# Q projection: weights by a cast on ScalarE from plain f32 loads instead of casting DMAs

## The reference

```python
x = x + attn(layernorm(x), Wq, Wk, Wv, Wo)      # 8192 tokens, H = 4096
x = x + ffn(layernorm(x), int4 gate, up, down)  # inner size 11008

# inside attn; 32 query heads, 8 key/value heads, head size 128
q = hidden_states @ Wq                          # [8192, 4096] @ [4096, 4096]
q = q * cos + rotate_half(q) * sin              # rotary embedding
# k, v alike; window of 512 past tokens; softmax; probs @ v; @ Wo
```

## Time and profile before

| what | us |
|---|---|
| median of the two runs shown | 10358.07 |
| the two runs | 10188.14 and 10528.0 |
| the profiled execution, its device time | 10198.96 |
| the profiled execution, span of its slowest core (core 2) | 10197.4 |
| spans of all cores in it | 10127.5 to 10197.4 |
| Q projection, first to last matmul start on core 2 | 3741.8 to 4577.9 |

### The profile page before, as it was taken

One profiled execution on the slowest core, in us unless ns is written; L12 is line 12 of the kernel. 1 busy time (PEld: TensorE's weight loads), 2 busy tenths in 40 slices (PEclk: granted clock), 3 DMA queues, 4 the chain that ended last, 5 costly groups with the idle time before them and its releaser, 6 DMA issues.

```text
span 10197.4 us, 80736 instructions; the slowest of 8 cores (10127.5 to 10197.4 us)
## 1 busy us (share of the span) xinstructions
PE 5936.4 (58%) x29632; PEld 2963.5 (29%) x29632; DVE 2148.5 (21%) x6972; ACT 2092.0 (21%) x4186; POOL 267.1 (3%) x316
## 2 busy tenths in 40 slices
PE   0000000332244566666657757999978879999886
PEld 0000000222222242221126633444433334444333
DVE  4555555444412112221100021000000000000000
ACT  3444444666603000004430031000000000000000
POOL 0000000000000001110000000000000000000000
PEclk9999999555566787776668868999989989999998
DMA  9999999999843334330024415777744467777333
GB/s 292 325 324 325 324 323 287 271 273 262 250 62 79 37 42 40 39 37 0 0 33 75 78 35 116 145 152 149 151 129 141 132 133 152 150 152 148 139 135 119
DMA packets 2257604, 1544.43 MB, mean 151 GB/s; under 512 B 1632064, under 2 KB 2095936, under 8 KB 2200640
## 3 DMA queue, kind: packets, MB, share of 16 engines
q1 hardware_dynamic: 1911968, 1134.47, 44.3%
q0 software_dynamic: 308096, 134.24, 9.9%
q10 hardware_dynamic: 37152, 270.55, 6.7%
HBM read 983.41 MB, written 295.70 MB: 125 GB/s over the span
## 4 chain that ended last, share of the span: by engine, by line
PE 50%; DMA 30%; DVE 7%; ACT 6%; issue 4%; SPq 2%; POOL 1%; ACTq 0%; DVEq 0%; POOLq 0%
PE pd L1074 12%; DMA scr_g<-wb_g 11%; PE pgg L1001 10%; PE puu L1009 10%; DMA qsl_d<-qd_in 7%; PE pq L679 5%; PE po L855 5%; DVE wb_g L247 3%; ACT wb_d L385 3%; DMA wq_sl<-wq_t 2%; DMA wgu_sl<-scr_u 2%; DMA x1t_sl<-scr_x1t 2%; PE pvv L569 2%; DMA wo_sl<-wo_t 2%; ACT probs L777 2%
## 5 line engine op out<-in xcount | busy, mean ns | idle before, releaser
L324 PE MATMUL ptd<-ident,wb_d 128*128 128x128 bf16 x2752 | 302.6, 308 | 2452.5 <-ACT wb_d L385 2452.5
L1074 PE MATMUL pd<-hT,wd_sl 128*128 128x512 bf16 x5504 | 1209.8, 383 | 258.6 <-DVE out_st L1090 238.2
L1001 PE MATMUL pgg<-x2nT,wgu_sl 128*128 128x512 bf16 x5504 | 1223.7, 381 | 108.5 <-DMA wgu_sl<-scr_u 99.0
L1009 PE MATMUL puu<-x2nT,wgu_sl 128*128 128x512 bf16 x5504 | 1216.0, 379 | 0.0
L324 PEld LDWEIGHTS ptd<-ident,wb_d 128*128 128x128 bf16 x2752 | 283.8, 145 | 2471.0 <-issue 2471.0
L276 ACT ACTIVATE wb_u<-qsl_u,nzs_u,s_u 128x128 bf16<-128x128 int32 x1892 | 737.0, 479 | 918.1 <-DMA qsl_u<-qu_in 918.1
L247 DVE TENSOR_SCALAR wb_g<-qsl_g,s_g,nzs_g 128x128 bf16<-128x128 int32 x2752 | 713.2, 344 | 732.5 <-DMA scr_g<-wb_g 730.2
L1074 PEld LDWEIGHTS pd<-hT,wd_sl 128*128 128x128 bf16 x5504 | 542.9, 99 | 925.5 <-issue 289.4
L1001 PEld LDWEIGHTS pgg<-x2nT,wgu_sl 128*128 128x128 bf16 x5504 | 536.4, 98 | 775.8 <-issue 146.3
L1009 PEld LDWEIGHTS puu<-x2nT,wgu_sl 128*128 128x128 bf16 x5504 | 538.6, 98 | 649.3
L679 PE MATMUL pq<-x1nT_o,wq_sl 128*128 128x512 bf16 x2048 | 522.0, 423 | 325.1 <-DMA wq_sl<-wq_t 325.1
(11 more groups left out here) (96 smaller groups left out, 3048.4 us busy)
## 6 DMA issues: line engine op xcount, KB each, us to landing
qsl_g<-qg_in SPq DMA_DIRECT2D x86, 2048.0 KB, 37.4
qsl_u<-qu_in SPq DMA_DIRECT2D x86, 2048.0 KB, 44.3
qsl_d<-qd_in SPq DMA_DIRECT2D x86, 2048.0 KB, 16.7
wd_sl<-scr_d SPq DMA_DIRECT2D x80, 2048.0 KB, 8.7
scr_u<-wb_u ACTq DMA_DIRECT2D x86, 1024.0 KB, 18.3
scr_g<-wb_g ACTq DMA_DIRECT2D x86, 1024.0 KB, 27.5
scr_d<-sst ACTq DMA_DIRECT2D x86, 1024.0 KB, 11.4
wq_sl<-wq_t POOLq DMA_DIRECT2D x128, 256.0 KB, 5.7
```

Source lines behind the costliest of these rows:

```text
L324: last = tensor.transpose(ptd[it % 2][:, hs * 128:(hs + 1) * 128], wb_d[it % 2][:, hs * 128:(hs + 1) * 128], ident[:])
L1001: last = tensor.matmul(pgg[it % 2][:], wgu_sl[2 * (it % 2)][:, ht * 128:(ht + 1) * 128], x2nT[:, ht * TOK + tc * 512:ht * TOK + (tc + 1) * ...
L1009: last = tensor.matmul(puu[it % 2][:], wgu_sl[2 * (it % 2) + 1][:, ht * 128:(ht + 1) * 128], x2nT[:, ht * TOK + tc * 512:ht * TOK + (tc + ...
L1074: last = tensor.matmul(pd[:, oi * 512:(oi + 1) * 512], wd_sl[(og * NGRP + grp) % 2][:, gi * 1024 + oi * 128: gi * 1024 + (oi + 1) * 128], ...
```

## The change

The host lays Wq out as [32 heads, 4 quarters, 128 partitions, 1024], so that what one partition needs of a quarter is one run of 4 KB. The loads move from GpSimd's queue to SyncE's and stay f32: each quarter is loaded in two halves of [128, 512] f32 (256 KB) into one of two staging tiles `wqf0` and `wqf1`. ScalarE copies each half into `wq_sl` and casts it to bf16 on the way. A load into a staging tile waits until the copy that read it two units earlier is done (`aQC`). The first copy of a head waits until both halves of the head before are done (`pQ`). TensorE waits for all eight copies of its head. GpSimd does nothing in this stage. The matmuls and the rotary embedding stay as they are.

```diff
-    wq_t = dram_in("wq_t", [NH, H, 128], F32)
+    wq_t = dram_in("wq_t", [NH, 4, 128, 1024], F32)
@@
     wq_sl = [P.sb(f"wq_sl{i}", [128, 8 * 128], BF16, OFF_G + i * 2 * KB) for i in range(4)]
+    wqf = [P.sb(f"wqf{i}", [128, 512], F32, OFF_G + 12 * KB + i * 2 * KB) for i in range(2)]
...
-    def p4_gp(gpsimd):
-        P.wge(gpsimd, "pVb", 32)
-        q = 0
-        for qt in range(NH):
-            for quarter in range(4):
-                if q >= 4:
-                    P.wge(gpsimd, "pQ", 2 * ((q - 4) // 4) + 2)
-                P.inc(gpsimd.dma_start(
-                    wq_sl[q % 4].ap().rearrange("p (t q) -> p t q", q=128),
-                    wq_t[qt].rearrange("(a t p) q -> a p t q", a=4, p=128)[quarter]),
-                    "lq%d" % (q % 4), 16)
-                q += 1
+
+    def p4_sync(sync):
+        P.wge(sync, "pVb", 32)
+        for u in range(8 * NH):
+            qt, a, hf = u // 8, (u % 8) // 2, u % 2
+            if u >= 2:
+                P.wge(sync, "aQC", u - 1)
+            P.inc(sync.dma_start(
+                wqf[u % 2][:],
+                wq_t[qt, a, :, hf * 512:(hf + 1) * 512]), "lqf%d" % (u % 2), 16)
+
+    def p4_sca(scalar):
+        P.wge(scalar, "pVb", 32)
+        for u in range(8 * NH):
+            qt, a, hf = u // 8, (u % 8) // 2, u % 2
+            P.wge(scalar, "lqf%d" % (u % 2), (u // 2 + 1) * 16)
+            if u % 8 == 0 and qt >= 1:
+                P.wge(scalar, "pQ", 2 * qt)
+            P.inc(scalar.activation(
+                wq_sl[a][:, hf * 512:(hf + 1) * 512],
+                wqf[u % 2][:], AF.Copy), "aQC")
 
     def p4_pe(tensor):
...
         for qt in range(NH):
-            for sl in range(4):
-                P.wge(tensor, "lq%d" % sl, (qt + 1) * 16)
+            P.wge(tensor, "aQC", 8 * (qt + 1))
             for ch in range(2):
...
-    bodies(tensor_f=p4_pe, vector_f=p4_vec, gpsimd_f=p4_gp)
+    bodies(sync_f=p4_sync, tensor_f=p4_pe, vector_f=p4_vec, scalar_f=p4_sca)
@@
-    wq_t = np.ascontiguousarray(wq.reshape(H, NH, 128).transpose(1, 0, 2))
+    wq_t = np.ascontiguousarray(
+        wq.reshape(4, 8, 128, NH, 128).transpose(3, 0, 2, 1, 4)).reshape(NH, 4, 128, 1024)
```

## The result

The changed kernel is slower by 0.84%: the ratio of its time to that of the kernel before is 1.0084, 95% interval 1.0062 to 1.0105, about 86 us. The medians over all runs are 10354.1 us (12 runs) and 10338.61 us (11 runs). They stand so close together because both hold runs in which the cores of a die were granted a lower clock; the ratios leave such runs out, and e8's profiled execution and cores 4 to 7 of e5's are of that kind. The profiled executions are 10264.51 us after and 10198.96 us before, 65.6 us apart.

What follows compares the result with a forecast made beforehand. TensorE and the Wq loads taking turns bound the changed stage. 31 gaps gave +36 us and the first head +3: 10198.96 plus 39 is 10238, 10245 with half of two upward bounds; range 10185 to 10400.

Steps and rivals of the forecast that it cites:

- The turn of TensorE and the loads: Q projection: with one set of weight tiles, TensorE and the loads alternate, a gap of 10.15 us a head before the change.
- three loads in a row in the gap: Between heads, loads 2, 4 and 6 stand one behind the other with copies between, each at its whole landing time.
- The load: One 256 KB f32 load issued by SyncE takes 2.4 us from issue to landing, read off the down weights' slope.
- my upper bound: Bound from above for one such load's landing: 3.25 us, from a 128 KB GpSimd read plus the other 128 KB.
- The copy and the handovers: In the gap: a 512-column ScalarE copy 0.61 us; handovers 0.08 us to a load, 0.16 after landing, 0.15 to TensorE.
- The sum of a gap: Gap between heads: three rounds of 3.25 us plus copies and handovers, 11.3 us against 10.15, +36 us for 31 gaps.
- The first head: No halves are loaded ahead, so its gap is 13.9 us against 10.56, +3 us.
- The clock: TensorE's granted clock in the Q projection: 0 us put, bound 0 to +0.8 us a head, 25 us in all.
- The total: Whole kernel: +39 us on the profiled 10198.96 us, giving 10238, or 10245 with half of two small upward bounds.
- A: Rival in the gap: small SyncE loads are slow, 4.1 us or more each, kernel over 2% slower; chance 0.12.
- B: Rival in the gap: loads take 1.5 to 1.9 us, gap 8.6 to 9.8 us, time 10151 to 10190; chance 0.12.
- C: Rival in the gap: prefetching two halves hides the rest, leaving 4.9 us of copies, time 10035; chance 0.02.

Runs made afterwards that it cites:

- e8: Kernel before with Wq's new layout and eight quarter tiles, each released and waited for by itself; comparable executions 9855.19 and 9848.15 us.
- e5: Changed kernel with the second staging tile loaded only once, so loads have no partner (wrong weights); stage 864.0 us, gap 11.7 us, no ratio.
- e1: Changed kernel with four f32 staging tiles instead of two; 10117.3 us, ratio to the kernel before 0.9917.
- e2: Changed kernel with six of each head's eight loads left out (wrong weights), one load still in the gap; 10105.22 us, gap 7.4 us.
- e10: Kernel before, its four tiles and layout kept, each quarter released and waited for by itself; 9841.27 us, no ratio, about 3.2% less by means.
- e4: Kernel before with only the new layout of Wq in DRAM, GpSimd's casting loads kept; 10138.81 us, ratio 0.9971.
- e9: Same kernel as e8, run again beside more runs of the kernel before; 9826.42 us, ratio 0.9611.

## Why the prediction was wrong, point by point

*The turn of TensorE and the loads; three loads in a row in the gap.* Right, and the chain of the changed kernel shows three loads in it, though loads 5 and 7 in place of 4 and 6. e1 confirms it by taking two of the three away.

*The load.* Wrong in size, and this is the step that failed. I took 2.4 us; the three on the chain shown took 2.87, 3.00 and 2.95, 2.94 in the mean (2.91 over the 97 loads on the chain of the whole stage, core 2). The number was about right for a load alone (e2: 2.42, median 2.5), but the chain never has one alone: load 3 is issued behind copy 1, while load 2 is on its way. My text saw the partner and allowed only for load 7 being "up to 0.3 us late" at the end of the gap, once. In the head shown load 7 held copy 7 up by 0.83 us, and the loads ahead of it were longer too. 0.54 us by three loads by 31 heads are 50 us, and 2 us more in the first head. e5 gives about 0.3 us of the 0.5 to the partner; the rest is open. The value stayed under the 3.25 us of my upper bound. The Trainium skill (DMA: Bandwidth & Descriptors, Anatomy of one DMA) gives its 2.0 us plus bytes at 436 GB/s as a fit for one DMA on GpSimd's path, not on SyncE's; the 2.6 us estimated by it lie between the 2.5 us of e2 and the 2.8 us median of the changed kernel, and say nothing of a neighbour under way.

*The copy and the handovers.* 0.64 us on the chain instead of 0.61; the two handovers of a round 0.06 and 0.08 us instead of 0.08 and 0.16. Together 0.07 us less a round than in the sum. From ScalarE's end to TensorE it was 0.25 us instead of 0.15.

*The sum of a gap.* 0.08 + 0.64 + 3 x (0.06 + 2.94 + 0.08 + 0.64) + 0.68 + 0.25 = 12.8 us against the predicted 11.3 and the measured 12.70 (0.68 for the one copy that follows another directly).

*The first head.* It waited 16.4 us instead of 13.9. Part of that is ahead of its first copy, in the chain and in ScalarE's timeline:

```profile
3734.53 0.75 ACT L671
3735.28 0.55 issue
3735.83 0.64 ACT wq_sl L671
```

```profile
3734.53 1.28 ACT L671 ACT_TABLE_LOAD   x1 [436.19 <-DMA wqf<-wq_t]
```

ScalarE loads its function table for 1.28 us, which I had not seen coming. In this stage it happens once and costs 1.3 us of 10264. The rest is the longer loads.

*The clock.* The granted clock of the stage is 0.77 (3731 to 4660 us) against 0.78, as good as unchanged. I had put 0 to +25 us on slow matmuls; they got 10.9 us shorter (522.0 to 511.1), so that small bound was on the wrong side (core 2). Why, no run shows.

*The total.* On core 2 the waits give +85.0 us (predicted +39) and the matmuls -10.9, together 74.1. Of that, 5.8 us are the longer first wait, ahead of the first matmul; the other 68.3 are the longer stage. Up to 3731 us the engines' busy times are the same to 2 us. Behind the stage core 2 takes back 9 us (its stage ends 74.8 us later, its span is 65.4 us longer). No cause is shown for them; in the mean of the cores all that lies outside the stage is 4 us shorter. The sum thus said +0.4% where +0.84% was measured. Within 2% was right, and the median of 10354 us lies between 10185 and 10400, though how far uneven executions lift a median is chance. The forecast was a change too small to tell, and the measured one is a clear, if small, loss, twice the sum. 10245 was made against an execution of 10199, and 1.0084 times that is 10285, which still lies inside the forecast's own 10190 to 10320. The 10245 also has a slip: half of the two upward bounds (9 and 25 us) is 17 us, so it should have read 10255. Beside medians of 10338 and 10354 the bare 10245 even reads like a gain, which the sum never said.

*The rivals.* A had the right sign and a far too high price: a load of 2.94 us, not 4.1 or more. B and C fell: no gap was shorter. What I had not listed is what e10 shows: the wait at the head's border was never needed at its full size. The change worked on what fills the gap, not on why there is one.

## What to carry to other kernels

When a ring feeds another single-buffered tile, count how many loads stand one behind the other between release and use, and price each at its landing time with its neighbours under way (here 2.9 us, not the 2.4 of one alone); the copies are the smaller part of such a chain (here five of 0.64 us in 12.7). Before building a staging path, look at what the consumer releases and when: letting go of each quarter after its own last matmul, and waiting for each quarter by itself, took out about 3.2% with four tiles, where the staging path lost 0.84%.

## What the runs showed that I had not expected

The landing time of a 256 KB load from SyncE depends on how many are under way: 2.5 us alone (e2), 2.6 in a row without partner (e5), 2.8 with one (changed kernel), 3.3 with four tiles (e1), all in the median of core 2. Runs of 4 KB in place of 512 B made GpSimd's issue shorter (0.55 us instead of 0.89) but not the landing of the last quarter behind its own issue (6.29 against 6.30 us, e4). And removing the waits of TensorE gave back more than the waits: 78 us of matmul time in e9, by the granted clock.
